# Dummy matrix products on TensorE at the head of six layer norms of a transformer stack

## The reference, cut to what matters

```python
def _layernorm(x, axis=-1, eps=1e-05):
    m = jnp.mean(x, axis=axis, keepdims=True)
    v = jnp.var(x, axis=axis, keepdims=True)
    return (x - m) / jnp.sqrt(v + eps)
...
    x = x + _L1_xattn_ref(_layernorm(x, axis=-1), ctx_1024, ctx_1024, mask_1x1xSxS2_ik1, ...)
    x = x + _L1_ffn_ref(_layernorm(x, axis=-1), ...)
```

## Time and profile before

| what | value |
|---|---|
| median of 3 runs | 2344.34 us (2340.66 to 2345.98) |
| the profiled execution | 2356.74 us |
| its span, first to last instruction | 2355.0 us |
| PE busy | 1682.6 us, 71% |
| PEld busy | 1190.1 us, 51% |
| DVE busy | 1580.0 us, 67% |
| ACT busy | 816.1 us, 35% |
| POOL busy | 902.3 us, 38% |
| mean granted TensorE clock | 0.794 |

### The profile page before, as it was taken

The page is one execution under the profiler, slowest core; times in us unless marked ns, Lnnn a source line. Parts: engine busy times, 40 slices in busy tenths (PEclk is TensorE's granted clock), DMA queues, the critical chain, the costliest instruction groups (busy, mean ns, idle before and its releaser), DMA issues. The chain is left out here.

```text
span 2355.0 us, 49069 instructions
## 1 busy us (share of the span) xinstructions
PE 1682.6 (71%) x14850; PEld 1190.1 (51%) x14853; DVE 1580.0 (67%) x3661; ACT 816.1 (35%) x1800; POOL 902.3 (38%) x1185
## 2 busy tenths in 40 slices
PE   3999943312399888995996799626998898158883
PEld 2777732011277655663785344214776677135552
DVE  4999963989767753446687899675555677763332
ACT  2544420334355422322563678400000564012221
POOL 1788810346234243014441000004554342018894
PEclk9999965555599988997998899857999898555555
DMA  3222200000000041111003477206774000214446
GB/s 110 66 65 66 63 2 26 0 0 1 7 1 0 15 153 39 41 37 33 1 0 64 180 304 304 104 0 201 284 286 153 2 0 28 86 42 78 77 78 139
DMA packets 178867, 184.55 MB, mean 78 GB/s; under 512 B 101410, under 2 KB 163682, under 8 KB 171234
## 3 DMA queue, kind: packets, MB, share of 16 engines
q1 hardware_dynamic: 155298, 114.23, 15.7%
q10 hardware_dynamic: 9152, 54.63, 6.4%
q0 software_dynamic: 14336, 14.69, 3.5%
HBM read 107.38 MB, written 72.45 MB: 76 GB/s over the span
## 5 line engine op out<-in xcount | busy, mean ns | idle before, releaser
L1920 POOL TENSOR_TENSOR gr_work<-gr_ring 128x512 f32<-128x512 f32 x96 | 121.7, 1280 | 398.3 <-DVE gr_part L1932 310.7
L748 DVE TENSOR_REDUCE at_mx<-at_psS 128x16 f32<-128x1024 f32 x96 | 117.6, 1225 | 95.3 <-PE at_psS L653 95.3
L711 ACT ACTIVATE at_ET<-at_psT 128x512 f32<-128x512 f32 x192 | 114.6, 597 | 172.0 <-PE at_psT L662 171.4
L617 POOL TENSOR_TENSOR at_KM<-at_K,at_mask 128x512 f32<-128x512 f32 x96 | 100.0, 1042 | 154.6 <-ACT at_Q L698 154.6
L1995 PEld LDWEIGHTS gr_psY<-gr_wd,gr_work 128*128 128x128 f32 x1024 | 132.0, 192 | 38.6 <-DVE gr_work L1955 23.9
L388 POOL TENSOR_TENSOR at_E<-at_Z,at_mx 128x512 f32<-128x512 f32 x128 | 130.9, 1044 | 51.2 <-DVE at_mx L513 51.2
L1995 PE MATMUL gr_psY<-gr_wd,gr_work 128*128 128x128 f32 x1024 | 139.9, 280 | 11.6 <-DVE gr_work L1955 11.6
L662 PE MATMUL at_psT<-kept_ident,at_Z 128*128 128x128 f32 x768 | 127.8, 290 | 9.1 <-DVE at_Z L761 5.0
L1844 PE MATMUL gr_psV<-kept_xT,gr_wu 128*128 (+1 forms) x256 | 126.7, 596 | 2.1 <-ACT gr_V L1698 2.1
L249 ACT ACT_TABLE_LOAD x6 | 7.7, 1283 | 346.6 <-PEq L63 331.0
L675 PE MATMUL at_psO<-at_VZ,at_ET 128*64 128x18 f32 x3072 | 107.0, 212 | 15.4 <-ACT at_ET L711 3.9
(11 more groups left out here) (562 smaller groups left out, 4700.2 us busy)
## 6 DMA issues: line engine op xcount, KB each, us to landing
gr_spill<-gr_ring SPq DMA_DIRECT2D x28, 1792.0 KB, 5.7
gr_ring<-gr_spill ACTq DMA_DIRECT2D x28, 1792.0 KB, 7.0
at_amask<-mask_Bx16xSxS_ff SPq DMA_DIRECT2D x128, 128.0 KB, 2.8
cap_acc<-cap_zero SPq DMA_DIRECT2D x2, 2112.0 KB, 12.5
cap_sums<-cap_acc SPq DMA_DIRECT2D x8, 512.0 KB, 7.3
ex_xs<-ex_zero SPq DMA_DIRECT2D x1, 2496.0 KB, 11.1
ex_row<-ex_xs SPq DMA_DIRECT2D x39, 64.0 KB, 1.8
ex_ys<-ex_out SPq DMA_DIRECT2D x39, 64.0 KB, 1.6
```

Source lines behind the costliest of these rows:

```text
L617: pool.tensor_tensor(KM[:, s, :, :], K[:, s, :].unsqueeze(1).broadcast_to([P, 4, P]), mask4[:, :].unsqueeze(2).broadcast_to([P, 4, P]), AL ...
L711: act.activation(ET[:, 4 * a:4 * a + 4, :].rearrange("p r q -> p (r q)"), psT[:, :], ACT.Exp, scale=QK_SCALE).then_inc(exped, 1)
L748: dve.tensor_reduce(mx[:, :].rearrange("p (g v) -> p g v", v=4), psS[:, :, 0:256].rearrange("p g (v k) -> p g v k", k=SEQ), AX.X, ALU.max) ...
L1920: pool.tensor_tensor(tp[:, s % 4, :], ring[:, s // 4, first, :], ring[:, s // 4, first + 1, :], ALU.mult).then_inc(pooled, 1)
```

## The change

At the beginning of TensorE's part of the block, ahead of its first wait, five f32 products are issued in each layer norm that transposes, ln0 excepted: ln2, ln3, ln4, ln5, ln6 and ln7. Each multiplies the identity with 512 columns of the context and writes to a PSUM bank of its own, `psD`, which nothing reads. They wait for nothing and nothing waits for them, but TensorE's transposes stand behind them.

```diff
@@ -179,6 +179,9 @@
         groups = NT // 4
+        warming = 5 if to_xT and part != "ln0" else 0
+        if warming:
+            psD = own.enter_context(nc.psum_tensor(part + "psD", [P, 512], F32))
 
@@ -264,6 +267,8 @@
             def _(pe):
                 if not to_xT:
                     return
+                for k in range(warming):
+                    pe.matmul(psD[:, :], m.ident[:, :], m.ctxT[:, 512 * k:512 * k + 512], start=True, stop=True)
 
                 def turn(g, u, n):
                     pe.wait_ge(hat_ready, g + 1)
```

## The result

The changed kernel takes 2350.47 us (median of 11 runs) against 2345.89 us for the kernel before (11 runs): ratio 1.0022, interval 1.0012 to 1.0032. It is about 5 us slower, which is little, but the interval leaves out no change. I had forecast +0.4 us and a range of 2335 to 2356 us.

A forecast was written before the change was run, and what follows sets the result against it. Norms start at TensorE's slow clock; VectorE and TensorE alternate in ln2, ln4, ln6, TensorE bounds ln3 and ln7, SP ends ln5. Terms +5.4 + 0 - 4.0 - 1.0 = +0.4 us on 2344.3 give 2344.7 us, range 2335 to 2356.

The forecast's parts named there:

- The price of the products: At the norms' heads, five products were to make the transposes start 3.3 us late, bounds 2.8 to 3.7 us.
- my 4.2: At the norms' heads, the clock was to rise 4.2 us into the products, the middle of 3.3 and 5.05 us.
- the term of 1.5 us given back: In ln2, ln4 and ln6 each, a clock staying up was to return 1.5 us of the 3.3 us lost.
- my first rival: In the norms, the clock rises but falls again over the transposes: +14.5 us in sum, 2359 us; chance 0.13.
- a forecast of -4.0: In ln7, the write wait covers most products and groups run faster: -4.0 us, bounds -4.9 and -2.5.
- my 1286.2: In ln5 before the change, VectorE's end at 1286.2, ahead of SP's 1288.7; the norm was costed at nothing.
- forecast at -1.0: In ln3, -1.0 us, the middle between -3.0 with the fast clock throughout and +1.0 if it falls.
- the +1.0 that I had for a clock that falls: In ln3, the cost of +1.0 us if the clock falls after two groups.
- The third rival: ln7 stays bound by its writes' return and gains only 1 us, ln3 loses 1: +5.4, 2349.7 us; chance 0.07.
- the second rival: The clock holds in ln3 and the block behind, and stays up ahead of ln6: -8.6, 2335.7 us; chance 0.23.
- My sign that blocks other than the norms change by more than 2 us: Outside the norms, a block changing by more than 2 us was to show the forecast wrong.
- The cover that the head gives: At each norm's head, TensorE's idle 3.2 us was to cover that much of the five products' work.

## Why the prediction was right in its range and 5 us off in its value

- The error has two parts. The value, 2344.7 against 2350.47, is off by 5.8 us, of which 1.6 lie in the kernel before, whose median is 2345.9 over eleven runs where I had 2344.3 from three. The change itself, +0.4 against +5.2 by the ratio (4.6 by the medians), is off by 4.8.
- The price of the products was right in the changed kernel's profile. At the head of ln2, ln4 and ln6 the transposes started 2.7, 3.2 and 2.9 us late (5.9, 6.4 and 6.1 us after the head's start, less 3.2); I had 3.3 with 2.8 to 3.7. The clock rose 3.0 to 4.0 us after the start in all six, against my 4.2. That profile was a good one: in each of the other kernels with five products at least one norm had its rise only 5.8 to 6.2 us after the start and its transposes up to 4.2 us late, beyond my bounds.
- The step that failed in mechanism is "my sum uses it for the pure transposes of ln2, ln4 and ln6 too", the term of 1.5 us given back. The clock held in ln5 and ln7, where routing products of 64 columns stand between the transposes, and fell 6.8 us after its rise in ln2, ln4, ln6 and ln3. Over all profiles with two or more products there, or forty transposes, ln5 kept it in eight of eight, ln7 in seven of nine and ln3 in none of nine. Given back were 0.8 us in ln2, 0.6 in ln4 and 0.8 in ln6. Instead of +5.4 us the three cost +6.6 (1.2 of the 4.8 us), which the run with products in them alone confirms (+6.6, 1.0017 to 1.0038 of the time). Pure transposes are on the edge: over the profiles of five kernels without fillers (five products, in all norms or in these three, forty transposes, two and three products) the clock was lost before the groups ended in ten of fifteen such norms and held in five. With a filler after each group, or after six of the eight, it held in twelve of twelve. This is my first rival in part: the fall came, but not because transposes don't count at all, since forty of them raised the clock and in five norms transposes alone kept it. What exactly the groups lack is not shown; it is not busy time alone, as ln3 tells.
- ln7 was right in size in the profile, -4.6 us against a forecast of -4.0, and in its mechanism on the whole: the wait for the write, which the norm had anyway, covered the products. Two smaller errors cancelled by luck. The third group's transposes came 8.28 us after the head's start (8.36 before) and not 9.2, and the five groups took 1.92 us each, (17.86 - 8.28) / 5, and not 1.73 to 1.85. In the mean it is worth less, -2.3 us when alone (-4.5 to -0.5), because the clock sometimes rises there by itself. With 1.7 us this is the largest miss among the terms. I had taken a single profile's 0.50 throughout for the norm's constant state.
- ln5 cost nothing that shows: SP ended the block in every profile with products there, and it lasted 22.7 to 23.8 us, where it lasted 22.6 to 23.6 in the five profiles without. In those VectorE was through 19.3 to 22.4 us after the head's start, so my 1286.2 was the early end of what it does, and in two of them VectorE and not SP ended the block.
- ln3 was forecast at -1.0; it came out at +0.2 in the profile (24.04 less 23.87), and +0.9 when alone, close to the +1.0 that I had for a clock that falls.
- The sum of the terms as measured one by one is 6.6 - 2.3 - 1.4 = +2.9 us, with the ln3 run's -1.4; the whole measured +5.2 (2.8 to 7.5). The intervals of the parts, about 2.3 us each, cover the difference. So 2.3 of the 4.8 us have no term that can be named.
- The third rival, +5.4 us, came nearest in number, and not by its reason: it had ln7 bound by its writes and gaining 1 us, and in the profile ln7's third group waits for no write.
- Two readings of mine were loose and change nothing: 818 us lies in a slice at 9 tenths, and only the slice from 824 us shows less; and the second rival's -5.9 for ln3 does not follow from its terms, -3.0 and -2.5, which make -5.5. My sign that blocks other than the norms change by more than 2 us was met by the experts and the grouped block, and both changes appeared between two profiles of the kernel before.
- The cover that the head gives was priced right, and the count of products is what the change got wrong. The table shows it, from the runs with the same edit and another count (eleven or twelve executions each, five for two products, each against its own executions of before).

| products at each head | ratio to before | interval | rise of the clock |
|---|---|---|---|
| 1 | 0.9997 | 0.9985 to 1.0008 | none at the heads |
| 2 | 0.9966 | 0.9952 to 0.9979 | 3.1 to 5.8 us |
| 3 | 0.9974 | 0.9964 to 0.9984 | 3.2 to 5.9 us |
| 5 | 1.0022 | 1.0012 to 1.0032 | 3.0 to 4.0 us, in other kernels with five up to 6.2 |

From two products to five the transposes of ln2, ln3, ln4, ln6 and ln7 start 2.3, 2.5, 2.8, 2.7 and 2.7 us later, 13.0 us in all, and the two ratios differ by 0.0056, which is 13.1 us. The five blocks are 2.6, 2.3, 2.4, 3.5 and 1.5 us longer, 12.3 in all. So what stands past the head is paid, in the sum though not norm by norm, and it buys no more of the clock: from the first transpose to the block's end of ln2, ln3, ln4 and ln6 the clock was up for 4.0, 4.2, 4.5 and 4.3 us with five products, 17.0 in all, and for 8.0, 3.4, 3.4 and 9.6 with two, 24.4 in all. The lowest ratio of the study is that of two products; three, and two with fillers (0.997), are not told apart from it.

## What to carry to other kernels

Dummy work that warms TensorE has a budget: the pause it stands in. Count what it costs at the slow clock, since that is the clock it meets, and stop where the pause ends; the real work behind it can finish the raising. Before crediting a stage with the fast clock, find a trace in which that very work keeps it, since neither a neighbour's work nor the busy share was a safe guide here, and look at more than one execution, for the clock that a stage gets can differ from one to the next.

## What the runs showed of the hardware that I had not expected

- Forty f32 transposes of 128 x 128, back to back, raised the clock 3.4 to 4.4 us after their start in the six norms, as five products did (3.0 to 4.0).
- The same transposes in the norm's own pace, two groups (eight transposes) in 2.4 us in ln2, kept the clock in five norms and lost it in ten; with one product of 256 columns after each group, or after six of the eight, it was kept in twelve of twelve.
- The busy share did not sort the stretches. The clock stayed at 0.50 for 10 us of an attention with TensorE busy for 10.00 us, and fell in ln3 behind 3.85 of 4.20 us; it stayed at 1.00 in ln6 with two products over 5.42 of 9.50 us.
- How late the clock rises in a block goes with the block's length. In the attentions behind ln4 and ln6 it rose 12.4 to 14.4 us after the start in most profiles, with blocks of 149.9 to 150.9 us (worked out from the timelines like the table above); at 11.4 us the block lasted 149.0, at 17.6 us 151.5, at 18.5 us 152.3, at 21.7 us 153.8 and at 27.8 us 155.6. The 18.5 us came in the kernel with products in ln3 alone, whose code at these blocks is that of before.
